# Additive masks with 64 contraction rows, first loads in four groups, and reordered stage transitions in a two-layer decoder with experts

## The chip, the cores and the metric

The kernel runs on one core of a Trainium2 chip. The metric is the device time of one execution in microseconds (us), as the median over several runs. The core has a matrix engine (TensorE, in the profile PE for products and PEld for weight loads), a vector engine (DVE), a scalar engine (ACT), GpSimd (POOL) and a queue that issues transfers (SyncE, SP). The matrix engine has two clock levels, 1.2 and 2.4 GHz, and the profile gives the granted one as a share of 2.4 GHz.

## What is computed

The input x has 8 items of 128 tokens with 256 features. Six sublayers follow each other, each of the form x = layernorm(x + f(x)); the kernel calls them A to F:

```python
x = _layernorm(x + _L0_attn_ref(x, ...))       # A: causal self-attention, 16 heads of 16
x = _layernorm(x + _L0_xattn_ref(x, ctx, ...)) # B: cross-attention on relu(linear) features
x = _layernorm(x + _L0_ffn_ref(x, ...))        # C: 64 experts of 96 units, top 8
x = _layernorm(x + _L1_attn_ref(x, ...))       # D: gated linear attention in chunks of 64
x = _layernorm(x + _L1_xattn_ref(x, ctx, ...)) # E: 32 query heads, 8 key heads, windows
x = _layernorm(x + _L1_ffn_ref(x, ...))        # F: 8 experts of 176, top 2, and a shared one of 704
```

Two of them mask their scores. A sets scores above the diagonal to minus infinity. E lets a query see two windows of keys, one of 64 tokens in one set of keys and one of 32 in the other, beside a linear bias:

```python
delta = -rel                                   # rel = key position - query position
ssm_mask = (delta >= 0) & (delta < W_SSM)      # 64
att_mask = (delta >= 0) & (delta < W_ATT)      # 32
scores = scores + bias[None]
scores = jnp.where(mask[None, None], scores, -jnp.inf)
wei = jax.nn.softmax(scores, axis=-1)
```

## The kernel before, in words

All activations stay on the chip. Each engine has its own program, written out by hand, and the engines meet on semaphores. A wait on an engine holds everything behind it on that engine. What is issued first is decided by the order of the calls in these programs.

**First loads.** The SP queue issues every transfer at L346, in lists called A, A2, B. A holds the whole transposed input (1 MB), a small head mask, all eight weights and biases of A, and two tensors of constants for `v` (a column of ones per head, 256 KB each); A2 holds the mask of A, two identities, the input by rows (1 MB). `loaded(engine, "A")` waits for the whole list: TensorE, ACT, DVE and POOL all begin with it.

**A and B** (`pe_self_cross`) are one software pipeline over 16 items: eight of A and then eight of B. Per step, TensorE projects keys, values and queries of one item, forms the scores of it (`scores`, L479 and L485), transposes the exponentials of another (L493), and multiplies with the values (L524). In A, `scores` first writes the mask into four PSUM banks: four products of the identity (128x128, bf16) with `causal` (512 columns), L479. The sixteen score products of 32 contraction rows at four tile positions (L485) accumulate onto it.

**C and F** (`pe_moe`) run over blocks of 128 hidden units: 48 in C and 17 in F. One block is `gate_up` (L995: for each half t of the tokens, a gate part s=0 and an up part s=1, six products of 512 columns each) and `down` (L1012: twelve products, six for each t). POOL splits each weight block into a high and a low part (L1977, L1979). Ahead of the loop the router decides the weights of the tokens: `pe_logits` (L960), a chain of small DVE instructions (`Router`), `pe_combine_T` (L970) for each half of the tokens, a copy by ACT into `cT`, and `pe_token_weights` (L981), which spreads them. As soon as both halves of `cT` are there, the SP queue writes them to DRAM, reads them back spread, issues the loads of all weights and constants of D and E (L320, in C only), and only then refills the four buffers of weight blocks (L284). Before its first `down`, TensorE clears the four output banks with products of the identity and a tile of zeros (L1030, four of 512 columns, bf16).

**D and E** (`pe_linear_cross`). D runs over eight items in 64x64 and 128x64 tiles. E then runs in iterations t of 12 steps k. In one iteration TensorE works for one item on `scores` (rows are queries, for the maxima that DVE takes) and for the item before it on `scores_T` (rows are keys, for the exponentials by ACT). Each call writes one PSUM bank of 512 columns: a mask product first (the identity with a mask, 128 contraction rows, bf16: L788 and L796 in `scores`, L829 and L836 in `scores_T`), and score products of 100 or 102 contraction rows on top. Every third step is a short one for the early queries: in `scores` four products of 128 columns (L792), in `scores_T` two of 256 (L832). The other eight steps have two products of 256 columns in each call (L799, L840). The order within a step is mask, scores, mask, transposed scores. Both calls run in seven of the nine iterations; the first has only `scores`, the last only `scores_T`.

## Time and profile before

| | |
|---|---|
| Median of 3 runs | 1089.61 us (1089.28 to 1089.79) |
| Profiled execution | 1087.74 us, of which the span from first to last instruction 1085.9 us |
| TensorE products | busy 993.8 us (92% of the span), 6139 instructions |
| TensorE weight loads | busy 785.1 us (72%), beside the products |
| DVE, ACT, POOL | busy 617.8, 430.2, 319.8 us |
| Mean granted clock of TensorE | 0.96 |
| Chain that ended last | TensorE 81%, transfers issued by SP 5%, DVE 5%, waiting for nothing visible 3% |

A product is shown with its contraction rows and output columns of the array (128\*128), its moving operand (128x512) and its type. Products are pipelined, and the profile models their ends; so two products are compared by their starts. A product of 512 columns of bf16 in a run of its own kind starts 0.216 us after the one before. Lines of code are lines of the kernel before.

### The profile page before, as it was taken

What the parts mean: (1) busy time and instruction counts of PE and PEld (TensorE: products, weight loads), DVE (VectorE), ACT (ScalarE), POOL (GpSimd) and SP (SyncE); (2) the same over time, 40 slices, a digit from 0 to 9 for tenths busy, and PEclk for the clock granted to TensorE, in tenths of its full rate; (3) what the DMA queues carried; (4) which work ended last, traced back from release to release, by engine and by line L of the source; (5) the groups of instructions that cost most, each with busy time, mean ns of one, the idle gap of its engine ahead of it and who ended that gap; (6) DMA issues with size and microseconds to landing.
All of it is one profiled execution on the core that took longest, in us unless ns stands there. A gap on an engine that the chain in (4) does not pass through costs nothing.

```text
span 1085.9 us, 18386 instructions
## 1 busy us (share of the span) xinstructions
PE 993.8 (92%) x6139; PEld 785.1 (72%) x6148; DVE 617.8 (57%) x1035; ACT 430.2 (40%) x839; POOL 319.8 (29%) x530
## 2 busy tenths in 40 slices
PE   4999997969999999999999689868999998999994
PEld 3778885658888888888888335557787776688883
DVE  2666777435555555555556457554555563455555
ACT  2777785413223223223222223224555554323221
POOL 0033124214443443443444301110000014234431
PEclk9999998989999999999999789978999999899998
DMA  8000000464333333333330000011111101264511
GB/s 298 2 2 2 2 2 2 94 177 140 129 115 117 110 111 119 107 110 120 109 106 15 9 1 1 17 27 27 25 25 31 32 11 59 59 183 106 120 31 39
DMA packets 36950, 75.74 MB, mean 70 GB/s; under 512 B 6844, under 2 KB 17960, under 8 KB 36498
## 3 DMA queue, kind: packets, MB, share of 16 engines
q1 hardware_dynamic: 36606, 74.77, 23.8%
q8 instruction: 34, 0.56, 0.2%
q0 software_dynamic: 288, 0.23, 0.2%
q14 instruction: 22, 0.18, 0.1%
HBM read 67.80 MB, written 2.40 MB: 65 GB/s over the span
## 4 chain that ended last, share of the span: by engine, by line
PE 81%; SPq 5%; DVE 5%; issue 3%; DMA 2%; ACT 2%; POOL 1%; DVEq 0%; POOLq 0%; ACTq 0%
PE ps L995 31%; PE ps L1012 15%; PE ps L411 4%; PE ps L628 3%; PE ps L418 3%; PE ps L493 3%; SPq L364 2%; SPq L320 2%; PE ps L861 2%; PE ps L485 2%; PE ps L524 2%; PE ps L745 1%; PE ps L836 1%; PE ps L840 1%; PE ps L796 1%
## 5 line engine op out<-in xcount | busy, mean ns | idle before, releaser
L995 PE MATMUL ps<-shared 128*128 128x512 f32 x1560 | 381.2, 394 | 9.5 <-POOL shared L1979 9.5
L995 PEld LDWEIGHTS ps<-shared 128*128 128x128 f32 x1560 | 296.9, 191 | 74.0 <-issue 11.7
L1397 ACT ACTIVATE shared<-pT 128x512 fp32r<-128x512 f32 x130 | 82.1, 632 | 287.4 <-DVE pT L1815 287.4
L1977 POOL CAST shared<-wraw 128x512 fp32r<-128x512 f32 (+1 forms) x130 | 92.0, 708 | 315.1 <-PE ps L1012 288.5
L1818 DVE TENSOR_TENSOR al<-pT,shared 128x512 fp32r<-128x512 f32 x130 | 117.1, 901 | 104.3 <-ACT shared L1397 104.3
L1012 PE MATMUL ps<-shared 128*128 128x512 f32 x520 | 162.4, 394 | 1.3 <-DVE al L1818 1.2
L1807 DVE TENSOR_TENSOR e<-e,ps 128x512 f32<-128x512 f32 x130 | 89.3, 687 | 128.4 <-PE ps L995 128.1
L1979 POOL TENSOR_TENSOR shared<-wraw,shared 128x512 fp32r<-128x512 f32 (+1 forms) x130 | 132.3, 1017 | 10.4
L1873 POOL TENSOR_SCALAR newton<-agg 128x1 f32<-128x1 f32 (+1 forms) x36 | 9.1, 254 | 384.1 <-DVE agg L1442 357.5
L1012 PEld LDWEIGHTS ps<-shared 128*128 128x128 f32 x520 | 98.4, 190 | 23.4 <-DVE al L1818 2.1
L1391 ACT ACTIVATE e<-ps 128x512 f32<-128x512 f32 x130 | 77.7, 597 | 84.3 <-PE ps L995 84.2
L1815 DVE TENSOR_TENSOR pT<-e,kbd 128x512 f32<-128x512 f32 x130 | 99.0, 761 | 10.0 <-DMA kbd<-combine_C 3.0
L1012 PE MATMUL ps<-al,shared 128*128 128x512 f32 x260 | 101.8, 392 | 0.0
L1012 PEld LDWEIGHTS ps<-al,shared 128*128 128x128 f32 x260 | 49.2, 189 | 10.3
L1458 DVE TENSOR_REDUCE mx<-ps 128x8 f32<-128x1024 f32 x32 | 39.0, 1220 | 22.2 <-PE ps L485 22.2
L1653 DVE TENSOR_REDUCE mcol<-ps 128x2 f32<-128x512 f32 x64 | 43.2, 677 | 6.0 <-PE ps L799 5.7
L411 PE MATMUL ps<-c_x_t,arena 128*128 128x128 f32 x192 | 28.2, 291 | 14.4 <-DMA v<-in_A_ones_v 12.4
L1137 ACT ACTIVATE pT<-ps 128x512 f32<-128x512 f32 x64 | 36.4, 598 | 8.0 <-PE ps L493 7.9
L799 PE MATMUL ps<-kT,shared 100*128 100x256 f32 x128 | 39.4, 391 | 0.0
L1466 DVE TENSOR_TENSOR e<-ps,mx 128x1024 f32<-128x1024 f32 x32 | 39.0, 1220 | 0.6
L411 PEld LDWEIGHTS ps<-c_x_t,arena 128*128 128x128 f32 x192 | 24.5, 197 | 20.3 <-DMA v<-in_A_ones_v 12.4
L1289 ACT ACTIVATE e<-ps 128x512 f32<-128x512 f32 x48 | 28.4, 595 | 26.6 <-PE ps L832 14.9
(225 smaller groups left out, 1447.5 us busy)
## 6 DMA issues: line engine op xcount, KB each, us to landing
kbd<-combine_C SPq DMA_DIRECT2D x46, 512.0 KB
wraw<-in_C_w SPq DMA_DIRECT2D x48, 384.0 KB, 8.1
kbd<-combine_F SPq DMA_DIRECT2D x15, 512.0 KB
wraw<-in_F_w SPq DMA_DIRECT2D x17, 384.0 KB, 7.1
kbd<-kbd SPq DMA_DIRECT2D x96, 32.0 KB, 1.9
kT<-kbd SPq DMA_DIRECT2D x48, 32.0 KB, 1.8
c_x_t<-in_x_t SPq DMA_DIRECT2D x1, 1024.0 KB, 4.9
c_x_rows<-in_x_rows SPq DMA_DIRECT2D x1, 1024.0 KB, 7.0
```

What stands on the lines that cost most here:

```text
L411: mm = pe.matmul(dst[:, c * P:(c + 1) * P], w[:, k, c * P:(c + 1) * P], src[:, k, :], start=(k == 0), stop=(k == C - 1))
L799: mm = pe.matmul(bank[:, o * D:(o + 1) * D], q_[0:KR, g, 1, o * P:(o + 1) * P], k_[t][0:KR], start=False, stop=True, skip_group_check=True)
L995: mm = pe.matmul(GU[t][s], w[u][:, (c * 2 + s) * P:(c * 2 + s + 1) * P], xx[:, c, t * HALF:(t + 1) * HALF], start=(i == 0), stop=(i == 5))
L1012: mm = pe.matmul(Y[:, 2 * m + t, :], w[u][:, (4 + m) * P:(5 + m) * P], x_[t][:, :], start=False, stop=False, skip_group_check=True)
L1391: act.activation(sgt[t], GU[t][0], ACT.Silu).then_inc(S("silu"), 1)
L1397: act.activation(ah[t][:, :], a2[t], ACT.Copy).then_inc(S("ah"), 1)
L1653: dve.reduce_max(m4[:, g0 + k % 3 - 1, 1, :], SRING[n % 2].rearrange("p (o k) -> p o k", o=2), AX.X)\
L1807: dve.tensor_tensor(a1[t], sgt[t], GU[t][1], ALU.mult).then_inc(S("m_a1"), 1)
L1815: dve.tensor_tensor(a2[t], a1[t], wbc[k][:, t * HALF:(t + 1) * HALF], ALU.mult)\
L1818: dve.tensor_tensor(al[t][:, :], a2[t], ah[t][:, :].bitcast(F32), ALU.subtract)\
L1977: pool.tensor_copy(wh[u][:, lo:hi], wraw[k][:, lo:hi]).then_inc(S("m_wh"), 1)
L1979: pool.tensor_tensor(wl[u][:, lo:hi], wraw[k][:, lo:hi], wh[u][:, lo:hi].bitcast(F32), ALU.subtract).then_inc(S("m_wl"), 1)
```

## The change

1. **Masks of E.** A mask product now contracts over 64 rows. Its stationary operand is 64x128 from a new constant `windows`, its moving operand 64 rows. The masks of `scores` lie on partitions 0 to 63 (tile position (0, 0)), those of `scores_T` on 64 to 127 (tile position (64, 0)). `scores` and `scores_T` are cut in halves h of 256 columns in the eight long steps. The order within a half is: mask of scores, mask of scores_T, score product, transposed score product. Per long step there are two pairs of masks of 256 columns, per short step one pair of 512.
2. **Masks of A.** Four products of 128 rows become eight of 64 rows and 64 output columns, at tile positions (0,0), (64,64), (0,64), (64,0).
3. **First loads** in groups A0 (input of two items, head mask, keys' weight and bias), A1 (values, queries), A2 (masks, identities, input rows of two items, output weight), A3 (the rest of the input). TensorE, ACT and DVE begin on A0, and wait for the later groups where they use them. The constants of `v` are no longer loaded; POOL writes them with four memsets. The biases of B are formed at step 6, not 2.
4. **Transitions.** Into C, the gate part of block 0 is issued a step earlier; the rest of `gate_up` of block 0 is spread around `pe_combine_T(1)`, which comes after 12 products and not after 24 (in F after 6, not 24). The clearing products of L1030 go: the first product into each bank starts it. The first `down` waits for two copies of token weights, not four. ACT is reordered to match.
5. Four mask tensors of E become one, so the SP queue issues three loads fewer at L320.

The diff, cut to its core:

```diff
-        XT = const("A", "x_t")
-        hmask = const("A", "head_mask")
-        causal = const("A2", "causal_bf16", BF16)
+        XT = sb("c_x_t", [P, C, T])
+        loads["A0"] = [(XT[:, :, 0:2 * P], a["x_t"][:, :, 0:2 * P])]
+        hmask = const("A0", "head_mask")
+        causal = [const("A2", f"causal{h}_bf16", BF16) for h in range(2)]
...
-        X = const("A2", "x_rows")
+        X = sb("c_x_rows", [P, B, D])
+        loads["A2"].append((X[:, 0:2, :], a["x_rows"][:, 0:2, :]))
+        loads["A3"] = [(XT[:, :, 2 * P:], a["x_t"][:, :, 2 * P:]), (X[:, 2:, :], a["x_rows"][:, 2:, :])]
...
-        for layer, names in (("A", "wq wk wv bq bk bv wo bo"),
-                             ("B", "wfc bfc wq wk wv bq bk bv wr"),
+        for group, names in (("A0", "wk bk"), ("A1", "wv bv wq bq"), ("A2", "bo wo")):
+            for n in names.split():
+                weight("A", n, group)
...
-        smask = [const("E", f"smask{h}_bf16", BF16) for h in range(2)]
-        tmask = [const("E", f"tmask{h}_bf16", BF16) for h in range(2)]
+        windows = const("E", "windows_bf16", BF16)
...
                     for r in range(4):
-                        pe.matmul(ps[:, r, :], ident16[:, :], causal[:, :], start=True, stop=False, skip_group_check=True)
+                        for n in range(2):
+                            rows, out = bass.ds(64 * n, 64), 64 * (n ^ r % 2)
+                            pe.matmul(ps[out:out + 64, r, :], ident16[rows, rows], bc(causal[r % 2][rows, :], 1, 4),
+                                      start=True, stop=False, tile_position=(64 * n, out), skip_group_check=True)
...
+                if t == 2 * B + 3:
+                    pe.wait_ge(S("pc"), 8 * B)
+                    pe_gate_up(pe, "C", 0, 0, 0, (0,))
...
-                    pe.wait_ge(S("pc"), 8 * B)
-                    pe_gate_up(pe, "C", 0, 0, 0)
...
+            def scores_mask(b, k, h):
...
+                if k % 3 == 0:
+                    pe.matmul(SRING[n % 2], windows[0:64, 0:P], bc(windows[0:64, P:2 * P], 1, 4),
+                              start=True, stop=False, tile_position=(0, 0), skip_group_check=True)
+                else:
+                    pe.matmul(SRING[n % 2][:, h * D:(h + 1) * D], windows[0:64, 0:P], windows[0:64, 2 * P:4 * P],
+                              start=True, stop=False, tile_position=(0, 0), skip_group_check=True)
...
+                lo, n_q, at_ = (0, 8, 0) if k % 3 == 0 else (P + h * P, 4, h * D)
+                pe.matmul(TRING[n % 3][:, at_:at_ + n_q * 64], windows[64:128, lo:lo + P],
+                          bc(ident16[64:128, 64:128], 1, n_q), start=True, stop=False, tile_position=(64, 0),
+                          skip_group_check=True)
...
-                    if es is not None:
-                        scores(es, k)
-                    if ev is not None:
-                        scores_T(ev, k)
+                    for h in range(1 if k % 3 == 0 else 2):
+                        if es is not None:
+                            scores_mask(es, k, h)
+                        if ev is not None:
+                            scores_T_mask(ev, k, h)
+                        if es is not None:
+                            scores(es, k, h)
+                        if ev is not None:
+                            scores_T(ev, k, h)
...
-            gate_up(0, 0, 1)
-            gate_up(1, 1, 0)
+            if L == "C":
+                pe_gate_up(pe, L, 0, 0, 0, (1,))
+            pe_gate_up(pe, L, 0, 0, 1, (0,))
             pe_combine_T(pe, BEFORE[L], 1)
+            pe_gate_up(pe, L, 0, 0, 1, (1,))
             pe_token_weights(pe, L, 0, 1)
             pe_token_weights(pe, L, 1, 1)
-            before_done(pe, L)
-            pe.wait_ge(S("zero16"), 1)
-            pe.wait_ge(S("m_spread"), 4 * (L == "F") + 4)
-            for m in range(4):
-                pe.matmul(Y[:, m, :], ident16[:, :], zero16[:, :], start=True, stop=False, skip_group_check=True)
+            gate_up(1, 1, 0)
+            pe.wait_ge(S("m_spread"), 4 * (L == "F") + 2)
             down(0, 0, 0)
             gate_up(1, 1, 1)
+            before_done(pe, L)
+            pe.wait_ge(S("m_spread"), 4 * (L == "F") + 4)
             down(0, 0, 1)
...
-            loaded(pool, "A")
+            for u in range(2):
+                pool.memset(v[u][:, :], 0.0).then_inc(S("v_one"), 1)
```

## Rows read from the trace of the kernel before

**Rows 1.** The page: its first line.
```profile
span 1085.9 us, 18386 instructions
```
**Rows 2.** Stages: length, busy (count) of PE, PEld, DVE, ACT, POOL; clock, DMA, GB/s.
```profile
811.00:834.00 23.00, 21.63 (x196) 17.93 (x195) 13.33 (x27) 12.38 (x25) 2.61 (x6) 1.00 0.13 29
...
907.00:945.00 38.00, 31.39 (x142) 21.71 (x143) 18.16 (x70) 13.15 (x30) 14.66 (x29) 0.87 0.16 30
```
**Rows 3.** Timeline of PE in E: start, length, line, tiles, shape, count [idle before].
```profile
801.89 0.38 PE L788 MATMUL ps<-c_smask_bf,c_ident_bf 128*128 128x512 bf16 x1
...
802.98 0.39 PE L796 MATMUL ps<-c_smask_bf,c_ident_bf 128*128 128x512 bf16 x1
...
803.91 0.39 PE L796 MATMUL ps<-c_smask_bf,c_ident_bf 128*128 128x512 bf16 x1
...
804.38 0.39 PE L836 MATMUL ps<-c_tmask_bf,c_ident_bf 128*128 128x512 bf16 x1
```
**Rows 4.** The same view in A, from masks to score products.
```profile
64.08 0.81 PE L479 MATMUL ps<-c_causal_bf,c_ident_bf 128*128 128x512 bf16 x3
64.82 0.71 PE L485 MATMUL ps<-kbd,qT 32*128 32x256 f32 x8
```
**Rows 5.** The same view in D, around a product of 33 contraction rows.
```profile
656.42 0.44 PE L671 MATMUL ps<-c_ident,an 128*128 128x128 f32 x2
656.79 0.50 PE L626 MATMUL ps<-shared 33*128 33x512 f32 x1
657.22 1.13 PE L628 MATMUL ps<-arena,c_x_t 128*128 128x512 f32 x2
```
**Rows 6.** A mask after a wait in E: its weight load, and its product.
```profile
757.61 0.10 PEld L788 LDWEIGHTS ps<-c_smask_bf,c_ident_bf 128*128 128x128 bf16 x1 [0.58 <-issue]
...
757.64 0.38 PE L788 MATMUL ps<-c_smask_bf,c_ident_bf 128*128 128x512 bf16 x1 [0.37 <-DMA kT<-kbd]
```
**Rows 7.** Waits in 811 to 834 us: total, times, longest.
```profile
PE ps L788 <- DVE shared L1637: 1.4, 1, 1.4
```
**Rows 8.** The chain that ended last: start, length, what.
```profile
6.31 6.07 DMA v<-in_A_ones_v
12.42 2.09 PE ps L411 x8
...
200.69 0.45 PE ps L970 x4
...
229.92 5.92 DMA wraw<-in_C_w
...
272.73 2.72 PE ps L995 x12
```
**Rows 9.** Transfers issued: source, queue, count, KB, us from issue to landing.
```profile
c_x_t<-in_x_t SPq DMA_DIRECT2D x1, 1024.0 KB, 4.9
```
**Rows 10.** Timeline of PE, DVE and SP into C.
```profile
184.94 0.69 PE L567 MATMUL ps<-c_ident,c_x_rows 128*128 128x128 f32 x2 [2.11 <-DVE c_x_rows L1518]
...
186.13 4.97 PE L995 MATMUL ps<-shared 128*128 128x512 f32 x12
...
196.51 0.42 DVE L1798 TENSOR_TENSOR oT<-oT,einv 128x256 f32<-128x256 f32 x1
...
227.44 0.90 SPq L320 DMA_DIRECT2D c_smask_bf<-in_smask_bf  x2
...
228.38 1.08 SPq L320 DMA_DIRECT2D c_tmask_bf<-in_tmask_bf  x2
...
238.26 4.55 PE L995 MATMUL ps<-shared 128*128 128x512 f32 x12 [9.49 <-POOL shared L1979]
```
**Rows 11.** Timeline of PE into F.
```profile
924.17 7.36 PE L995 MATMUL ps<-shared 128*128 128x512 f32 x24
...
935.80 1.49 PE L1030 MATMUL ps<-zero,c_ident_bf 128*128 128x512 bf16 x3 [1.16 <-ACT kbd L1381]
...
943.17 0.62 PE L1012 MATMUL ps<-shared 128*128 128x512 f32 x2
```

More of the change, by code:

```diff
@@ L65, in build, with weight @@
         filled = {"AB": 0, "DE": 0}
-        def weight(layer, name):
+        def weight(layer, name, group=None):
             src = a[f"{layer}_{name}"]
@@ L126, in build @@
         mx = [sb(f"mx{u}", [P, 8]) for u in range(2)]
-        for u in range(2):
-            loads["A"].append((v[u], a["A_ones_v"]))
         v3 = [x[:, :].rearrange("p (h w) -> p h w", w=VW)[:, :, 0:DH0] for x in v]
@@ L346, in load_weights @@
                     sp.dma_start(t[tuple(slice(None) for _ in t.shape)], src).then_inc(S(f"{L}_loaded"), 16)
-            load_weights("A")
-            load_weights("A2")
+            for group in ("A0", "A1", "A2", "A3"):
+                load_weights(group)
             load_weights("B")
@@ L794, in scores @@
                 else:
[L795 to L801 removed]
+                    mm = pe.matmul(bank[:, h * D:(h + 1) * D], q_[0:KR, g0 + k % 3 - 1, 1, h * P:(h + 1) * P],
+                                   k_[t][0:KR], start=False, stop=True, skip_group_check=True)
+                if k % 3 == 0 or h == 1:
+                    mm.then_inc(S("E_sps"), 1)
             def maxima_T(b, r):
@@ L834, in scores_T @@
                 else:
[L835 to L842 removed]
+                    mm = pe.matmul(bank[:, h * D:(h + 1) * D], k_[t][0:KM, (1 - h) * P:(2 - h) * P],
+                                   q_[0:KM, g0 + k % 3 - 1, 1], start=False, stop=True, skip_group_check=True)
+                if k % 3 == 0 or h == 1:
+                    mm.then_inc(S("E_sts"), 1)
             def values(b, r):
@@ L990, in pe_gate_up @@
                 pe.wait_ge(S("m_a1"), nm(L, 2, x * 2 + t - 1))
-            for s in range(2):
+            for s in parts:
                 i = 0
@@ L1010, in down @@
                 for m in range(C):
-                    for w, x_ in ((wh, ah), (wl, ah), (wh, al)):
+                    for i, (w, x_) in enumerate(((wh, ah), (wl, ah), (wh, al))):
                         mm = pe.matmul(Y[:, 2 * m + t, :], w[u][:, (4 + m) * P:(5 + m) * P],
-                                       x_[t][:, :], start=False, stop=False, skip_group_check=True)
+                                       x_[t][:, :], start=(first(x) and i == 0), stop=False, skip_group_check=True)
                 mm.then_inc(S("m_down"), 1)
@@ L1891, in residual @@
                     loaded(pool, "A2")
+                if L == "A" and b == 2:
+                    loaded(pool, "A3")
                 if L == "B" and b == 0:
@@ L1900, in residual @@
                     .then_inc(S("xb"), 1)
-            loaded(pool, "A")
+            for u in range(2):
+                pool.memset(v[u][:, :], 0.0).then_inc(S("v_one"), 1)
+            pool.wait_ge(S("v_one"), 2)
+            for u in range(2):
+                pool.memset(v[u][:, :].rearrange("p (h w) -> p h w", w=VW)[:, :, DH0:DH0 + 1], 1.0).then_inc(S("v_one"), 1)
             residual(0)
@@ L2022, in constants @@
     c["head_mask"] = (np.arange(P)[:, None] % 32 // DH0 == np.arange(2)[None, :]).astype(np.float32)
-    c["causal_bf16"] = bf16(np.tile(np.where(k > q, big, np.float32(0)), (1, 4)))
+    causal = np.where(k > q, big, np.float32(0))
+    c["causal0_bf16"], c["causal1_bf16"] = bf16(causal), bf16(np.roll(causal, 64, 0))
     def window(q, tokens, width):
```

116 lines of the change are left out of this document (52 added, 64 removed).

## The prediction, made before the change was run

> **What bounds the kernel now.** I read the table of stages first, then the chain that ended last, then the waits in E, then the timeline of TensorE where the change touches it. TensorE is the bound nearly everywhere: 81% of the chain is on it, and in an iteration of E (23 us) it is busy 21.6 us [rows 2]; the only wait of a product there that counts is 1.4 us, at the first short step [rows 7]. So an edit of TensorE's stream in A or E is worth what it does to that stream. There are three exceptions. The kernel begins with 12.4 us in which TensorE waits for list A of the loads; the last of its transfers was issued at 6.31 us and took 6.07 us [rows 8]. In C, TensorE stands still for 9.49 us until POOL has split a refilled weight block, and what POOL waits for hangs on the SP queue, which began its work when both halves of `cT` were there [rows 8, 10]. Into F there are small waits and a low clock: 0.87 over 38 us [rows 2, 11]. The span is 1085.9 us [rows 1], the profiled execution 1087.7 us, the median 1.9 us above that; the sum is made on the span, and the same difference is added to 1089.6.
>
> **Masks of E, the large term.** Before, a call's half of a step (one mask, 512 columns, and two score products of 256) takes 0.47 us (803.91 to 804.38) [rows 3]. Score products run at 0.227 us for 512 columns [rows 8], so the two take 0.24 and the mask 0.23. A long step with both calls takes 0.94 us. If a pair of masks in opposite halves of the rows runs at once, as four products at other tile positions do (L485, eight of them inside 0.71 us) [rows 4], a step saves one mask, 0.23 us.
>
> Against this stands the switch between tiles. The last causal mask starts at 64.08 + 2 x 0.216 = 64.51 and streams until 64.73; the first product of 32 rows, and its weight load with it, begin only at 64.82: 0.09 us in which nothing flows, though no wait is shown [rows 4]. The same holds where only the rows differ: L626, with 33 contraction rows, starts at 656.79 and L628, with 128, at 657.22: 0.43 us for a product that takes 0.227 in a run of its kind, so 0.20 for the switch [rows 5]. The way into L626 costs 0.09 too: the second product of L671 starts about 0.17 after the first and streams 0.11, to 656.69 [rows 5]. The 0.20 splits into 0.09 of standing still and 0.11 of a weight load that is otherwise hidden. A bf16 mask's weights come quicker: product 0.03 after its load [rows 6]. So the way into a mask costs 0.12, the way out 0.20. Score products have 100 and 102 rows and so use the whole array; before, mask and scores were of one kind and none of this was paid.
>
> The Trainium skill says the same in "TensorEngine Tiling (Array Packing)", section Tiling Modes: changing the mode, not just the tile, drains the engine. The trace agrees, with 0.09 us each time [rows 4, 5]. The same page's Overview gives up to 2 times for a contraction of at most 64; by that alone the masks would halve, which is the first rival below.
>
> Long step, per half h, after: 0.12 into the masks, 0.11 for the pair of 256 columns, 0.20 out of them, 2 x 0.117 for a score product of each call: 0.665 us; two halves 1.33, so 0.39 more than 0.94. Short step: before 1.09 (801.89 to 802.98) [rows 3]; after 0.12 + 0.22 + 0.20 + 4 x 0.11 + 0.235 = 1.21, so 0.12 more. An iteration with both calls: 8 x 0.39 + 4 x 0.12 = 3.6 us. Off this go 0.3, because in three places the stream changes tiles next to a mask already (values twice, keys and values once), and 0.4, because the 1.4 us of waiting [rows 7] hangs on a DVE chain that starts with the short step k=9 and has longer to run: 2.9 us each, 7 x 2.9 = 20.3. The last iteration has only one mask per pair, so nothing is saved: a long step of `scores_T` goes from 0.47 to 2 x (0.12 + 0.107 + 0.20 + 0.117) = 1.09, a short one gains 0.30: 8 x 0.61 + 4 x 0.30 = 6.1, less 0.7 of switches and waits that are there already: 5.4. In the first iteration TensorE waits for DVE and for transfers of the next keys anyway; only what is ahead of these keys counts: 2.0. Sum for E: **+27.7 us**. Bounds: a mask's weight load with 64 rows is not in the trace; between 0.03 and the 0.11 of the other kind this adds up to 0.08 for each of 160 groups of masks, 12 us. Downward, DVE and ACT have slack and could hide nothing more of a TensorE stream than the waits already in it; I allow 8 us for these. E lies between +19 and +41. New waits are added too: the transposed mask's wait for ACT stands ahead of the score product that DVE needs. Banks come round two and three steps later, so I cost it at nothing; what hides it is ACT's 12.4 busy of 23 us [rows 2], and a price would be at most some 0.3 us a step.
>
> **Masks of A.** Before 4 x 0.216 = 0.86 us per item [rows 4]. After, if all four tile positions run at once, 0.09 + 0.06 + 2 x 0.213 = 0.58; the way on to L485 costs what it did. 8 x 0.27 = **-2.1 us**. Here two tiles of different rows write one bank, which no row shows: with one after the other it is 8 x 0.213 + 0.1 = 1.8, so +7.6 us at the other end. I take the first, as L485 shows tiles together [rows 4].
>
> **First loads.** A0 is 0.5 MB in four transfers, issued by 2.7 us. The 1 MB of x_t was there 4.9 us after its issue at 0.9 us [rows 9], so half of it is there at about 5 us, and TensorE starts at 5.0 instead of 12.4: **-7.4 us**. A1 is needed 1.9 us after the start, but queries wait for ACT anyway. A2 (fifteen transfers in, some 2 MB) lands near 10.5, needed near 11. A3 has 7 us to spare. If A1 or A2 is late, up to 3 us are given back. POOL's four memsets lie in the time of loading. Moving the biases of B takes away a DVE wait that would otherwise have appeared; nothing gained.
>
> **Into C.** The end is set by the SP queue, so what counts is when the second half of `cT` is written. Before, `pe_combine_T(1)` ran at 200.69 [rows 8], though its DVE input was ready at 196.93 [rows 10]. After, 12 products fewer stand ahead (2.7), and six were moved into the 2.11 us hole before 184.94, out of the group that ran at the low clock (4.97 for twelve) [rows 10]; that brings the router's DVE chain forward by some 1.5 us, so the input is ready near 195.4 and the transposes run at about 196: 4.6 us sooner. Behind it the four mask loads took 2.0 us to issue [rows 10]; one is left: 1.4. The refill at 229.92 [rows 8] and the product at 238.26 [rows 10] move by **-6.0 us**. The clearing products of C cost nothing already: the wait of 9.49 behind them grows by what they free. Bounds -3 and -7.
>
> **Into F.** Here TensorE sets the pace. Before, from 924.17 to 943.17, it did 24 + 6 + 12 products of 512 columns in 19.0 us, with the clearing, a wait of 1.16 [rows 11] and one of 0.7 for `cT`, half of it at the low clock. The 24 took 7.2 us up to the next group where 24 x 0.227 is 5.4, so some 8 went at half speed, 3.4 us. After, the waits are covered by products: the same 3.4 us for the first 8, then 34 x 0.227 = 7.7, and 2.8 for transposes and token weights (0.6, and four long products at 0.43 with their switches): 13.9: **-5.1 us**. If the clock drops as before, 2 less. Bounds -2 and -6.
>
> **Sum.** -7.4 - 2.1 - 6.0 - 5.1 + 27.7 = +7.1. Span 1093.0, median 1089.6 + 7.1 = 1096.7 us.
>
> **Rivals.**
> 1. *The switch is not paid around masks of 64 rows.* Then E saves 0.23 for each of 84 pairs of masks, -19.3, and the total is -40: 1050 us. For it: nothing in the rows. Against it: 0.09 at every change of rows or columns [rows 4, 5]. It decides at the first pair: half a step would take 0.36, not 0.67.
> 2. *E loses less and the rest gains all it can* (not slower): each iteration pays 1.9 instead of 2.9 because the waits of 1.4 us [rows 7] vanish wholly, and C and F give 7 and 6: +19 - 22.5 = -3.5 to -6: 1085 us. It turns where E costs less than 20.6 us.
> 3. *Masks' weight loads take 0.11, or the masks of A go one by one*: +7 to +12 more: 1106.
> 4. *Less flows per microsecond in E and the clock falls.* A tenth of the 200 us of E at the low clock would add most of 20 us: 1115. Against it: it was 1.00 in 811 to 834 [rows 2].
>
> **How the numbers follow.** Forecast 0.61, own range 1087 to 1105. Rival 1: 0.14. Rival 2: 0.12. Rival 3: 0.10. Rival 4: 0.03. The range 1079 to 1111 takes in rival 3 and most of rival 2, and leaves out rival 1 and the far end of 4. A measurement can tell 0.2% or 2.2 us, so faster is below 1087.4 and slower above 1091.8. Faster: rival 1 and 0.11 of rival 2, 0.25; same: 0.01 of rival 2 and 0.11 of the forecast, 0.12; slower: the rest of the forecast 0.50, rivals 3 and 4 0.13, together 0.63.
>
> **What would show it.** In the changed profile: a long step of E with both calls near 1.33 us from pair to pair, with 0.09 us of nothing before the masks' and the scores' weight loads; iterations of 26 us and not 23; TensorE's first product near 5 us; the product after the refill wait near 222.8 (7.4 + 2.1 + 6.0 before 238.26); one stretch of low clock into F where there were two. The prediction is wrong if a pair costs under 0.4 us with both ways, if the start is later than 8 us, or if the refill wait in C grows by what was gained ahead of it.

## The result and the profile after

The changed kernel takes 1117.07 us (median, 1111.67 to 1119.68), the kernel before 1089.44 beside it: a ratio of 1.0257 with a 95% interval of 1.021 to 1.0303. That is 27.6 us slower, where the forecast was 7.1 slower and the range ended at 1111. A second comparison gave 1.0264 (1.0235 to 1.0293). So the direction was right and the size was not.

The page of the changed kernel, its first lines (columns as in [rows 1, 2]; the last line is TensorE's granted clock in 40 slices):

```profile
span 1115.8 us, 18701 instructions
...
PE 1049.1 (94%) x6300; PEld 788.7 (71%) x6300; DVE 621.5 (56%) x1034; ACT 432.6 (39%) x839; POOL 319.9 (29%) x534
...
PEclk9999996989999999999998699779889998899998
```

The span by stage shows where the time went. Each line is one stretch: its length, then busy time and count for PE, PEld, DVE, ACT and POOL, then the clock, the share of DMA, GB/s. The five stretches are: first product to the first token weights (A and B); from there to D's first numerators (C); to the products of keys and values in E's first iteration with scores, some 8 us behind its first mask (D); to the first token weights of F (E); and to the last products (F). The kernel before:

```profile
12.40:192.80 180.40, 170.21 (x1705) 138.25 (x1712) 121.31 (x208) 127.78 (x275) 47.03 (x128) 0.98 0.08 28
192.80:639.40 446.60, 422.51 (x1802) 337.15 (x1803) 244.32 (x346) 131.18 (x217) 174.16 (x214) 0.96 0.34 103
639.40:717.00 77.60, 67.83 (x447) 40.23 (x448) 52.69 (x95) 22.42 (x56) 10.42 (x36) 0.93 0.04 9
717.00:922.30 205.30, 185.14 (x1558) 150.41 (x1556) 109.25 (x236) 100.91 (x211) 29.25 (x72) 0.97 0.12 30
922.30:1073.30 151.00, 147.74 (x630) 118.97 (x632) 82.56 (x126) 47.95 (x80) 54.45 (x65) 0.97 0.38 90
```

The changed kernel:

```profile
5.58:186.40 180.82, 171.70 (x1739) 138.66 (x1739) 121.48 (x207) 127.86 (x275) 47.22 (x128) 0.97 0.11 39
186.40:634.40 448.00, 428.01 (x1805) 340.35 (x1804) 244.37 (x346) 131.43 (x217) 173.02 (x213) 0.95 0.35 102
634.40:712.70 78.30, 69.53 (x448) 40.36 (x449) 52.73 (x95) 22.42 (x56) 10.43 (x36) 0.92 0.03 9
712.70:955.70 243.00, 233.44 (x1684) 151.92 (x1682) 112.86 (x235) 103.08 (x211) 29.23 (x72) 0.89 0.09 26
955.70:1103.20 147.50, 146.08 (x627) 117.34 (x628) 82.71 (x126) 47.85 (x80) 54.38 (x65) 0.98 0.38 92
```

The first product comes 6.8 us sooner (12.4 to 5.58). E takes 37.7 us more, at a clock of 0.89 where it was 0.97. F takes 3.5 less. C, which was to gain 6, gains nothing (446.6 and 448.0). A second profiled execution of the changed kernel showed 0.89 in E too.

Three of E's iterations, as windows (columns as before); [rows 2] has 23.00 us at a clock of 1.00 for the same work:

```profile
793.39:821.97 28.58, 27.75 (x213) 18.32 (x212) 13.85 (x27) 12.60 (x26) 2.61 (x6) 0.88 0.09 23
821.97:849.20 27.23, 26.40 (x212) 17.49 (x212) 13.84 (x27) 12.61 (x26) 2.61 (x6) 0.94 0.10 24
849.20:876.47 27.27, 26.44 (x212) 17.50 (x212) 13.83 (x27) 12.60 (x26) 2.61 (x6) 0.94 0.10 24
```

The timeline of PE (TensorE's products) within E, halves of a long step (start, length, line, tiles, shape). L798 and L842 are the two masks, L812 and L856 the score products of the two calls:

```profile
786.41 0.39 PE L798 MATMUL ps<-c_windows_bf 64*128 64x256 bf16 x1
...
787.47 0.39 PE L798 MATMUL ps<-c_windows_bf 64*128 64x256 bf16 x1
...
806.51 0.28 PE L798 MATMUL ps<-c_windows_bf 64*128 64x256 bf16 x1
806.52 0.28 PE L842 MATMUL ps<-c_ident_bf,c_windows_bf 64*128 64x256 bf16 x1
806.73 0.39 PE L812 MATMUL ps<-kT,shared 100*128 100x256 f32 x1
806.95 0.28 PE L856 MATMUL ps<-shared,kT 102*128 102x256 f32 x1
807.16 0.28 PE L798 MATMUL ps<-c_windows_bf 64*128 64x256 bf16 x1
```

The two masks of a pair start 0.01 us apart, so they do run at once. From pair to pair it is 0.65 us (806.51 to 807.16), where the prediction had 0.665 and the kernel before 0.47 [rows 3]. The first two lines are the same half step inside a stretch of low clock: 786.41 to 787.47, 1.06 us. By the windows above, each of these iterations now has such a stretch, of 6.8 us at first and of 3 to 4 in the later ones; before, the clock was 1.00 there.

### The profile page after: what moved, and what is told of

Same layout as the page of the kernel before. It is cut to its first block, busy times and chain, and to the rows that moved or that the text cites. A ratio compares the mean times of both kernels' runs of the same rounds, so it can differ in the third digit from the quotient of the medians.

```text
span 1115.8 us, 18701 instructions
## 1 busy us (share of the span) xinstructions
PE 1049.1 (94%) x6300; PEld 788.7 (71%) x6300; DVE 621.5 (56%) x1034; ACT 432.6 (39%) x839; POOL 319.9 (29%) x534
## 4 chain that ended last, share of the span: by engine, by line
PE 85%; DVE 5%; SPq 4%; issue 2%; DMA 2%; ACT 1%; POOL 1%; DVEq 0%; POOLq 0%; ACTq 0%
PE ps L1017 30%; PE ps L1034 15%; PE ps L411 4%; PE ps L636 3%; PE ps L812 3%; PE ps L878 3%; PE ps L500 3%; PE ps L418 2%; PE ps L798 2%; PE ps L492 2%; SPq L320 2%; PE ps L809 2%; PE ps L531 2%; PE ps L856 2%; SPq L364 1%
## 5 line engine op out<-in xcount | busy, mean ns | idle before, releaser
L812 PE MATMUL ps<-kT,shared 100*128 100x256 f32 x128 | 53.3, 416 | 0.0
L842 PE MATMUL ps<-c_ident_bf,c_windows_bf 64*128 64x256 bf16 (+1 forms) x160 | 49.9, 312 | 1.4 <-DMA shared<-mlo 1.4
L1313 ACT ACTIVATE e<-ps 128x512 f32<-128x512 f32 x48 | 28.7, 598 | 40.5 <-PE ps L856 23.4
L1313 ACT ACTIVATE pT<-ps 128x512 f32<-128x512 f32 x48 | 28.7, 597 | 35.1 <-PE ps L856 21.2
L856 PE MATMUL ps<-shared,kT 102*128 102x256 f32 x128 | 39.5, 308 | 0.0
L500 PE MATMUL ps<-c_ident,e 128*128 128x128 f32 x256 | 38.3, 285 | 1.2 <-ACT pT L1161 0.8
```

Source lines behind the costliest of these rows:

```text
L500: mm = pe.transpose(PT[h][:, q * P:(q + 1) * P], e[u][:, at_:at_ + P], ident[:, :])
L812: mm = pe.matmul(bank[:, h * D:(h + 1) * D], q_[0:KR, g0 + k % 3 - 1, 1, h * P:(h + 1) * P], k_[t][0:KR], start=False, stop=True, skip_gro ...
L856: mm = pe.matmul(bank[:, h * D:(h + 1) * D], k_[t][0:KM, (1 - h) * P:(2 - h) * P], q_[0:KM, g0 + k % 3 - 1, 1], start=False, stop=True, sk ...
```

## Experiments

Every version stands beside the kernel before on the same chip. The first four were on a chip where the kernel before took 1087.60 us, the next four (the parts alone and the first of the versions with one change of tiles per long step) on one where it took 1087.18, the other four on one where it took 1085.13. Ratios are to these, with 95% intervals.

### Without E's masks

```diff
-    windows = const("E", "windows_bf16", BF16)
+    smask = [const("E", f"smask{h}_bf16", BF16) for h in range(2)]
+    tmask = [const("E", f"tmask{h}_bf16", BF16) for h in range(2)]
...
-    for h in range(1 if k % 3 == 0 else 2):
-        ... scores_mask, scores_T_mask, scores, scores_T
+    if es is not None: scores(es, k)
+    if ev is not None: scores_T(ev, k)
```

> The changed kernel with the masks of stage E, and the order of their products, as they were before the change; the loads in groups, the transitions and the masks of stage A as changed. Theory: all of the loss is in E, where the trace of the changed kernel shows +38.4 us between the start of E's loop and F; without it 1117.07 - 38.4 = 1078.7 us, 10.7 below before, and the middle iterations of E take 23.0 us again. Rival 1, the rest gains the whole of what the prediction summed (20.6 us) and E's masks interact with it: 1069 us. Rival 2, part of the loss belongs to the new transitions (a shifted phase of the clock into E): 1085 us or more, with E's iterations above 23.5 us.

Measured: 1070.26 us, ratio 0.9826 (0.9796 to 0.9857). E is back at its old length, so the loss sits in E's masks and the order of their products:

```profile
709.80:915.20 205.40, 185.23 (x1558) 150.49 (x1556) 109.23 (x235) 100.94 (x211) 29.25 (x72) 0.97 0.12 30
```

The rest gains 18.9 us by the ratio, which lies at rival 1's value (20.6) more than at the theory's 10.7. The profiled execution, 1075.5 us, was the slowest of its five, and by its stages it gains 12.2.

### E's masks alone

The reverse: the kernel before with the changed code of `windows`, `scores_mask`, `scores`, `scores_T_mask`, `scores_T` and the loop over halves.

> The kernel before with the new masks of stage E and the new order of their products alone. Theory (price of the switch between kinds of tiles, and the lower granted clock that follows in E): +38 us, 1127 us, middle iterations of E at 27 to 29 us, of which some 2 to 3 us of difference come with each stretch of low clock. Rival, the switch's price alone, as the prediction had it: +27.7, 1117 us, middle iterations near 26 us.

Measured: 1126.19 us, ratio 1.0333 (1.0297 to 1.037), 36.2 us slower. E by stages:

```profile
725.70:969.50 243.80, 236.37 (x1683) 154.67 (x1681) 112.11 (x235) 103.05 (x211) 29.29 (x72) 0.88 0.10 26
```

243.8 us, as in the changed kernel (243.0). From the first mask of one iteration to that of the next it is 30.3, 27.2, 27.2 and 27.3 us, 28.0 in the mean; in the changed kernel the same four take 28.6, 28.6, 27.2 and 27.3, 27.9 in the mean. (The profiled execution, 1135.6 us, was the slowest of six, 9 us above the median. Its A and B took 185.9 us where they had taken 180.4; its E agrees with the changed kernel's.) The rest of the change has no part in E's loss. The theory's 38 holds, the prediction's 27.7 does not.

### The new order and halves with masks of 128 rows

```diff
-    pe.matmul(SRING[n % 2][:, h * D:(h + 1) * D], windows[0:64, 0:P], windows[0:64, 2 * P:4 * P],
-              ..., tile_position=(0, 0), ...)
+    pe.matmul(SRING[n % 2][:, h * D:(h + 1) * D], ident16[:, :], smask[1][:, :], ...)
```

and so for the transposed masks.

> The changed kernel with its order and its halves, but the masks of E as products of 128 rows from the whole array (same count of instructions, same columns, the old tensors). Theory, the price lies in the switch between products of 64 rows and of more: no stop of 0.09 us before a weight load, half a long step 0.45 to 0.47 us, iterations 23 to 23.4 us, 1078 to 1081 us in all. Rival, the price lies in the order (a mask and its product apart, four weight loads in place of pairs): half a long step stays at 0.65 us, iterations at 27 us, 1115 us.

Measured: 1081.91 us, ratio 0.9933 (0.9904 to 0.9963). E and one half step (the same four products as above; mask to mask 816.38 to 816.85):

```profile
708.70:924.10 215.40, 194.76 (x1683) 155.53 (x1681) 110.41 (x235) 100.90 (x211) 29.37 (x72) 0.93 0.12 29
```

```profile
816.38 0.28 PE L799 MATMUL ps<-c_smask_bf,c_ident_bf 128*128 128x256 bf16 x1
816.50 0.27 PE L843 MATMUL ps<-c_tmask_bf,c_ident_bf 128*128 128x256 bf16 x1
816.53 0.36 PE L813 MATMUL ps<-kT,shared 100*128 100x256 f32 x1
816.73 0.28 PE L856 MATMUL ps<-shared,kT 102*128 102x256 f32 x1
816.85 0.28 PE L799 MATMUL ps<-c_smask_bf,c_ident_bf 128*128 128x256 bf16 x1
```

With as many products in the same order, half a step takes 0.47 us again: here the masks follow one another, and still it is 0.18 quicker than with the two at once. So the price lies in going from masks of 64 rows to products of 100 or more and back. (The two versions also differ in the masks' tile position and tensors. The doubled pairs of the next run, where further masks of 64 rows cost about their columns, speak against a price of the masks by themselves.) The order is not wholly free, though: E is 10.0 us longer than without E's masks, at a clock of 0.93 and not 0.97, where two middle iterations held the full clock and took 23.4 us (0.4 more). What in the order lowers the clock elsewhere, the halves or the transposed mask's wait that now stands ahead of the scores, was not tried apart. Here too the low stretches in the middle of E, 781 to 784 and 853 to 856 us, stand right behind the wait at the head of an iteration (1.5 us), but behind three other such waits there is none.

### Each pair of masks twice

```diff
     scores_mask(es, k, h)
     scores_T_mask(ev, k, h)
+    if es is not None and ev is not None:
+        scores_mask(es, k, h)
+        scores_T_mask(ev, k, h)
```

> The changed kernel with each pair of E's mask products issued twice in a row, where scores and transposed scores both run (the second pair writes the same values again; no further switch of tiles, 0.107 us more of columns per half of a long step, 0.21 per short step, 1.9 us per iteration at full clock, 7 iterations). Theory, the low clock in E comes with the share of time in which TensorE stands between the tiles: more columns per switch hold the clock up, iterations near 27.2 us all, +1 to +6 us on the changed kernel: 1118 to 1123 us. Rival, the low clock comes from the one long wait at the start of each iteration alone: it stays as it is and the columns come on top, +14 us or more at the mixed clock: 1131 to 1134 us.

Measured: 1121.02 us, ratio 1.0303 (1.027 to 1.0336), and one of E's iterations:

```profile
815.60:843.50 27.90, 27.51 (x252) 17.46 (x251) 13.79 (x27) 12.59 (x25) 2.61 (x6) 1.00 0.09 24
```

The expectation miscounted the columns added: an iteration has eight long steps and four short ones, so it is 8 x 2 x 0.107 + 4 x 0.213 = 2.6 us and not 1.9. Seven iterations would then cost 18 us; by the two ratios they cost 4 (1.0303 against 1.0264). The clock is why: it stands at 1.00 in every iteration from the third on, where the changed kernel had 0.88 to 0.94. An iteration here is 28.0 us, of which TensorE waits 0.4. So 27.6 less 2.6, and the 0.8 that it waits in the changed kernel, make some 25.8 us for an iteration of the changed kernel at full clock; it took 27.2 to 28.6. This run changes two things at once: it adds columns, and as these give VectorE more time, it also halves the wait at the head of the iteration (0.83 to 0.39 us). Which of the two holds the clock it can't say; the rival, that the clock stays low and the columns come on top, fell.

### The parts alone

The kernel before with the loads in groups alone, with the two transitions alone, and with A's masks alone.

> The kernel before with its first loads in four groups (and the ones in v written by POOL) alone. Theory: TensorE starts 6.4 to 6.8 us sooner and keeps it, as no later wait takes it up: -6.5 us against the kernel before. Rival, the gain is taken back by the wait for the second group and for the masks' load within the first items: -3 us or less.

Measured: 1079.43 us, ratio 0.9929 (0.9903 to 0.9955): -7.7 us. The first product is at 6.25 us, 6.2 sooner than before; the interval, -10.5 to -4.9, is too wide to tell 7.7 from that.

> The kernel before with the reordered transitions into C and F alone. The prediction had -6.0 (into C) and -5.1 (into F), -11.1 us. Theory, from the trace of the changed kernel, where stage C's steady loop began no more sooner than the first loads and the masks of A account for, and F came out 3.5 us shorter: -5 us, all of it in F, because into C the freed time is spent at low clock and on the weights' transfer. Rival, the prediction's terms were right and the change in E's masks hid them: -11 us, with both stages shorter by 5 to 6 us.

Measured: 1083.25 us, ratio 0.998 (0.995 to 1.001): -2.2 us, between -5.4 and +1.1. Its stretches of A with B, of C, and of F:

```profile
12.10:198.20 186.10, 175.86 (x1706) 142.22 (x1706) 121.50 (x207) 127.78 (x275) 46.97 (x128) 0.94 0.07 27
198.20:639.90 441.70, 422.09 (x1805) 338.16 (x1804) 244.72 (x346) 131.49 (x218) 173.41 (x213) 0.97 0.35 104
...
921.40:1069.00 147.60, 146.06 (x626) 117.03 (x627) 82.93 (x128) 47.93 (x81) 54.44 (x65) 0.98 0.39 92
```

F is 3.4 us shorter. A to C together take 627.8 us, before 627.0: nothing was gained into C. The end of B ran at a lower clock here, 0.65 over 170 to 195 us; in the kernel before it was 0.86. A mean as low is no mark of the new order: with E's masks alone, whose instructions in B are those of before, it was 0.55 (in the slowest of its six executions). The time from the first product to the first write of `cT` to DRAM was 189.4, 189.7, 195.0 and 189.0 us in the four profiled kernels with the old transition. In the ten profiled executions with the new one it lay between 186.5 and 195.3, with a median of 188.7; nine of these have A's new masks too, worth some 2, and their median is 187.7. So this stretch differs by several us from one execution to the next, and the reordering gives next to nothing, not the 4.6 of the prediction.

> The kernel before with the new masks of stage A alone. The prediction had -2.1 us (8 items, 0.28 us each). Theory, from the trace of the changed kernel (0.63 us for the eight products in place of 0.86): -1 to -2 us. Rival, the other end of the prediction's bounds, where the products of 64 rows do not run beside each other or the clock falls: +5 us.

Measured: 1085.47 us, ratio 0.9984 (0.9963 to 1.0005): -1.7 us, which is the prediction's -2.1 within what can be told, but by the interval (-4.0 to +0.5) no gain at all is possible too; the timeline, shown further down, decides.

### One change of tiles per long step

```diff
-    for h in range(1 if k % 3 == 0 else 2):
-        if es is not None: scores_mask(es, k, h)
-        if ev is not None: scores_T_mask(ev, k, h)
+    if es is not None: scores_mask(es, k, 0)      # 512 columns
+    if ev is not None: scores_T_mask(ev, k, 0)    # two products of 256
+    for h in range(1 if k % 3 == 0 else 2):
         if es is not None: scores(es, k, h)
         if ev is not None: scores_T(ev, k, h)
```

> The changed kernel with the masks of a whole long step (512 columns of each) ahead of its products, one change of tile kinds per step where there were two. Theory, the loss in E goes with the number of changes between kinds: per both-iteration 6 x (0.97 - 0.94) + 3 x 0.12 = +0.5 us at full clock, +3 us in the last iteration, +1 in the first, and 0 to 10 us of low clock as in the version with 128 rows: 1078 to 1090 us, middle iterations near 23.6 us. Rival, the loss comes from products of 64 rows as such (their own duration or their weight loads), not from the changes: as much as in the changed kernel, 1113 us or more, middle iterations at 27 us.

Measured: 1106.94 us, ratio 1.0186 (1.0156 to 1.0216). In this version the mask of one half of the transposed scores is lost. So it was run once more with the second transposed mask product as `start=(at_ == 0)`, which keeps it.

> As whole_steps, one change of tile kinds per long step, but the second of the two products that write a transposed mask doesn't begin its bank anew. Theory: a product that begins anew lets the products after it write over what the same bank's other half held, so in whole_steps one mask was lost, with no effect on time; here it is kept, and the time is the same: 1105 to 1109 us, E's iterations 23.6 us plus half of the low clock's 6.8 us. Rival: the lost mask was a sign of products that ran into each other, and the time changes with it by 5 us or more.

Measured: 1103.77 us, ratio 1.0167 (1.0137 to 1.0196), and an iteration of E:

```profile
815.50:842.40 26.90, 25.48 (x203) 17.18 (x203) 13.64 (x27) 12.29 (x26) 2.61 (x6) 0.87 0.10 25
```

So a product that starts its bank anew decides how later products treat what stands elsewhere in that bank, and the time hardly changes (3 us by the medians, on two chips, intervals that overlap). The Trainium skill, "PSUM — Partial Sum Buffer", section The four PSUM rules, states it so: the region that a starting product resets is the whole 2 KB bank, whichever part it writes; the two versions here agree with it. Neither theory of the first expectation holds whole: 1078 to 1090 us was expected if the loss went with the number of changes, 1113 or more if it did not. The loss falls by 8 to 11 us (1.0264 to 1.0186 and 1.0167) with half of the long steps' changes of tiles gone. At full clock the iteration would be 26.9 less half of the 6.8 us of low clock that it holds, 23.5, as expected (8 x 0.03 + 4 x 0.12 more than 23.0 is 23.7). But the clock is 0.87, no better than with twice as many changes: TensorE stands at the head of the iteration for 1.42 us (26.90 less 25.48), where it is 0.83 in the changed kernel. That the longer wait, together with the changes of tiles that remain, is what keeps the clock down is argued from this, and not tried in this version.

### The wait at the head of an iteration, filled

The waits of PE in the changed kernel, 780 to 900 us (line, releaser: total in us, times, longest):

```profile
PE ps L795 <- DVE shared L1664: 4.2, 5, 0.8
```

Each iteration begins with one wait of 0.8 us for VectorE's masked queries ([rows 7] had 1.4), and the low clock begins at it or up to some 2 us behind it, in all five iterations. The timeline and the window that follow show the first of the five:

```profile
784.80 0.37 PE L795 MATMUL ps<-c_windows_bf 64*128 64x512 bf16 x1 [0.83 <-DVE shared L1664]
```

```profile
785.90:792.70 6.80, 6.80 (x42) 3.10 (x41) 3.04 (x5) 1.94 (x4) 0.19 (x1) 0.50 0.02 5
```

The experiment puts four products of 512 columns ahead of that wait; their output is written over by the mask.

```diff
     if k == 0:
+        for _ in range(4):
+            pe.matmul(SRING[n % 2], ident16[:, :], bc(ident16[:, :], 1, 4), start=True, stop=False, ...)
         pe.wait_ge(S("E_k0st"), b * 48 + 48)
         pe.wait_ge(S("E_qm"), b * 2 + 1)
```

> The changed kernel itself, beside the next three on one chip. Theory (the parts add up: -18.9 us without E's masks, +36.2 for E's masks alone): ratio 1.016 to 1.02. Rival (the parts make each other worse by a further 10 us, as 1117.07 against 1070.26 us has it): ratio 1.025 or more.

Measured: 1112.64 us, ratio 1.0264 (1.0235 to 1.0293), which is +25.5 to +31.8 us. The theory's 1.016 to 1.02 fell; the number is the rival's, but not for its reason, since the four parts alone add up to -7.7 - 2.2 - 1.7 + 36.2 = +24.6, just below this interval and each with an interval of its own (2 to 4 us to either side). It is the version without E's masks that stands out by 7 us against the sum of its own three parts (-18.9 against -11.6, with intervals that just meet); nothing in its trace names a cause.

> The changed kernel with four products of 512 columns (0.85 us, written over afterwards) issued ahead of the wait with which each iteration of E begins (0.5 to 0.9 us, for VectorE's masked queries). Theory: the lower clock in E comes with the share of time that TensorE stands, and this wait is where that share is largest; filled, the clock holds as in the version with doubled pairs, the iterations take 25.5 us, and 7 x 1.7 = 12 us are gained less up to 3 for products that outlast the wait: 1104 to 1110 us where the changed kernel takes 1117. Rival: the stops at the changes of tiles alone are enough to lower the clock; iterations stay at 27 to 28.5 us, no gain or up to 3 us lost: 1115 to 1120.

Measured: 1100.09 us, ratio 1.0133 (1.0107 to 1.016), 12.5 us less than the changed kernel beside it, with 32 products more. One iteration (the next took 25.70 us too), and the whole of E with the fill and, from the execution of the changed kernel beside it, without:

```profile
785.40:811.10 25.70, 25.70 (x216) 17.26 (x215) 13.82 (x27) 12.59 (x25) 2.61 (x6) 1.00 0.10 26
...
711.80:939.10 227.30, 223.50 (x1711) 147.07 (x1709) 112.61 (x235) 102.84 (x211) 29.21 (x72) 0.97 0.10 28
```

```profile
707.60:950.00 242.40, 233.73 (x1684) 153.15 (x1682) 112.25 (x236) 103.06 (x211) 29.49 (x72) 0.89 0.10 26
```

The clock is 0.97 over E, as it was before the change, and E is 15.1 us shorter. This separates the two parts of E's loss: 22.0 us (227.3 - 205.3) for the switches, and 15.1 for the clock. Both are differences between single profiled executions, good to a few us. Not tried was the same filling elsewhere in the iteration; so that the wait is covered, and not only that more columns flow, rests on the wait's place right ahead of each low stretch.

### The refill ahead of the loads of D and E

The version without E's masks, in which SP issues C's first four refills of weights before the loads of D and E and not after them:

```diff
-    for M in ("D", "E"): ...            # loads of D and E, 21 transfers
+    for k in range(NW):
+        refill(1, k)
+    for M in ("D", "E"): ...
-    with sp.Fori(1, BLOCKS[L] // NW) as j:
+    with sp.Fori(1 + (L == "C"), BLOCKS[L] // NW) as j:
```

> The version without E's masks (no_e_masks) in which SP issues stage C's first four refills of weights ahead of the loads of D and E, instead of behind them. Theory: what the reordered transition into C could gain is taken by TensorE's wait of 9.2 us for the refill, which stands behind 22 to 25 us of those loads' issues on SP's queue; with the refill ahead the wait goes, and so 5 to 9 us: 1061 to 1065 us where no_e_masks takes 1070. Rival: the refill waits for VectorE, ScalarE or POOL to free the buffer, or for the transfer itself, and the order on SP changes nothing: 1070 us; or D's weights now come late, 1072 us or more.

Measured: 1062.33 us, ratio 0.9789 (0.9749 to 0.9828). The SP queue into C in the version without E's masks, from D's first load to the refill, and the product that waits for its data:

```profile
198.44 0.34 SPq L321 DMA_DIRECT2D arena<-in_D_wqk  x1
...
221.23 0.35 SPq L285 DMA_DIRECT2D wraw<-in_C_w  x1
...
229.26 5.44 PE L1004 MATMUL ps<-shared 128*128 128x512 f32 x12 [9.17 <-POOL shared L1998]
```

and with the refill ahead, with C's stretch:

```profile
201.41 0.35 SPq L285 DMA_DIRECT2D wraw<-in_C_w  x1
...
223.82 2.39 SPq L333 DMA_DIRECT2D arena<-in_D_wqk  x1
```

```profile
185.20:621.70 436.50, 421.25 (x1806) 338.02 (x1805) 244.94 (x345) 131.31 (x218) 173.82 (x213) 0.97 0.34 105
```

The refill goes out 19.8 us sooner, the wait of 9.17 is gone (one of 2.73 for a later block of weights takes its place), and C takes 436.5 us in place of 449.0. It is the quickest version of this study: 22.8 us less than the kernel before. Against the version without E's masks, run on another chip, the medians differ by 8 us while the intervals of the ratios overlap, so the step between the two rests on the traces.

## Why the prediction was wrong, point by point

**Switch between tiles (the kernel of the E term): right.** Half a long step was predicted at 0.665 us and took 0.65. With the wait filled, an iteration of 25.7 us holds 0.85 of filling; its work without that grew to 24.85 from the 21.63 of [rows 2], by 3.2, where the prediction had 3.3. Rivals 1 (no switch price) and 2 (E loses less) fell at the first pair, and rival 3 did too: mask weights cost no more than assumed, and A's masks run at once. (The 0.227 us that the prediction gives for score products is read from products of C [rows 8]; nothing in the sum turned on it.) For A, the timeline shows it, from the transposes ahead of the masks; before, with the score products at 64.82 [rows 4], and changed:

```profile
62.93 1.10 PE L493 MATMUL ps<-c_ident,e 128*128 128x128 f32 x8
```

```profile
65.57 1.10 PE L500 MATMUL ps<-c_ident,e 128*128 128x128 f32 x8
66.60 0.63 PE L485 MATMUL ps<-c_causal_bf,c_ident_bf 64*64 64x512 bf16 x8
67.15 1.15 PE L492 MATMUL ps<-kbd,qT 32*128 32x256 f32 x16
```

From the start of the transposes to the first score product it was 1.89 us and is 1.58: 0.31 less per item where 0.27 was forecast. Eight products of 512 columns pass in the 0.55 us from the first mask to the first score product.

**The sum over iterations in E: somewhat high.** 27.7 was predicted at full clock, and 22.0 remain with the wait filled. By the starts of the first mask of each iteration, the first one (scores only) takes 26.7 us with the fill and took 24.7 before, 2.0 more as forecast. The last, transposed scores only, was forecast at +5.4 and took 4.9 more (15.1 to 20.0 us from the last score product to the last transposed one). The seven with both calls take 15.2 more together where 20.3 was forecast. The miss is in the first two of them, 24.8 and 25.4 us with the fill, 23.8 and 25.7 before: there the kernel before waits for transfers and runs some 7 and 3 us at the low clock, and the filled one hardly does either. The prediction granted such waits to the first iteration only.

**The clock in E: the step that failed.** The prediction read 1.00 in [rows 2] and took the clock as given, with 0.03 for rival 4, "less flows per microsecond in E and the clock falls". That is what happened: +15.1 us. The rival's mechanism and its price (most of 20 us) were right, its chance was not. The change takes columns out (one mask of two) and puts stops in; both are in the prediction's own sum, and the kernel before already had 1.4 us of waiting in each iteration [rows 7]. The sum counted the stops as time and not as idle TensorE. Doubled masks, with half of the wait, and a filled wait each brought the clock in E's middle back to 1.00 without taking one change of tiles away. The wait alone did not lower the clock in the kernel before, where it was longer (1.4 us). With masks of 128 rows in the new order, so without a stop at the tiles, it did (1.5 us) in some iterations. So the low clock follows the wait, and the changed stream around it makes it fall there; how much of that the stops at the tiles do is not shown.

**First loads, -7.4: right within what can be told.** -7.7 alone; the first product came at 5.58 us in the changed kernel and 6.25 with the loads alone, where 5.0 was forecast.

**Masks of A, -2.1: right.** -1.7 alone, and 8 x 0.31 = 2.5 us by the timeline above.

**Into C, -6.0: wrong, about 0.** Both terms of it failed. The first is "12 products fewer stand ahead (2.7)" of the last transposes of `cT`, with what follows from it, "4.6 us sooner". It took products at full clock that in the new order run at the low one. The chain that ended last, before and changed (start, length, what; the transposes stand next):

```profile
192.83 1.98 PE ps L981 x4
194.81 5.88 PE ps L995 x24
```

```profile
186.46 3.71 PE ps L1003 x4
190.16 5.40 PE ps L1017 x12
```

The four products of the token weights take nearly twice as long, and twelve products of 512 columns almost as long as 24 did. It is so in all ten profiled executions with the new order: 3.7 us for the four and 4.1 to 5.3 for the twelve, by their starts. In the four with the old order it is 1.9 for the four and 5.8 for the 24. The transposes were to run 0.6 us after their input was ready; they ran 3.6 us after it in each execution of the old order and 3.2 to 4.3 in those of the new. What makes the low clock stay on there was not tried.

The second term is the 1.4 us for three mask loads less. They do shorten the queue: from the write of `cT` to the issue of the refill it is 27.2 us in the mean of the six profiled executions that load four masks and 25.6 in the seven that load one. But the refill then takes 5.4 us to land in the former and 7.1 in the latter, so that it is there 32.7 us after the write in both.

The product behind the refill wait, forecast at 222.8 us, stands at 231.29, 7.0 us sooner than before, of which the earlier start is 6.8 (the changed kernel):

```profile
231.29 5.36 PE L1017 MATMUL ps<-shared 128*128 128x512 f32 x12 [7.28 <-POOL shared L2011]
```

The other half of the reading was right: the SP queue sets C's start, as the refill put ahead showed. What the prediction wrote as its own test, that it is wrong "if the refill wait in C grows by what was gained ahead of it", did not come true either: the wait went from 9.49 to 7.28 us, and nothing was gained ahead of it.

**Into F, -5.1: near.** 3.4 alone, 3.5 in the changed kernel, 5.1 without E's masks. The clock over the first 19.3 us of F was 0.82 in the changed kernel:

```profile
955.70:975.00 19.30, 19.30 (x63) 12.80 (x64) 10.79 (x33) 8.44 (x16) 5.26 (x8) 0.82 0.30 56
```

The waits are covered (PE is busy throughout) and there is one stretch of low clock where there were two, as forecast; but 0.82 over 19.3 us means some 7 us at half speed where the forecast had 3.4. That is the case which the prediction priced at 2 less, and it came out at 1.7 less.

**The sum.** By terms, predicted and measured: E +27.7 and +37 (22 of switches, 15 of clock); loads -7.4 and -7.7; A's masks -2.1 and -1.7; C -6.0 and about 0; F -5.1 and -3.5. The measured terms give +24, the comparison 27.6. The switches came out 5.7 us cheaper than forecast, which hid a part of the clock's 15.1; without that luck the miss would be larger still. The two large misses are one kind of mistake: both took the clock that the kernel before shows at a place as a constant of that place, while the change itself moved it.

## What to carry to other kernels

Count what a change does to TensorE's idle share, not only to its time: fewer columns together with more stops lowered the granted clock here, and then products that were not touched are slower too. Two masks at once in opposite row halves gain 0.11 us per pair of 256 columns here, and the way into the tile kind and out of it costs 0.3 together. So it pays only where many such products follow each other, or where tiles change at that place anyway, as in A, whose masks always stood beside products of 32 rows. Ahead of a steady loop, look at what stands in front of its first refill on the issuing queue before reordering the engine that waits for it.

## What the runs showed of the hardware

- Idle TensorE cost more than its time. Four superfluous products per iteration (0.85 us) in a wait of 0.8 us made the iteration 1.5 to 2.9 us shorter (27.2 to 28.6, then 25.7), with the granted clock at 1.00 in place of 0.88 to 0.94.
- Two products of 64 contraction rows in opposite halves, with all 128 columns each and different banks, start within 0.01 us of each other; eight of 64x64 tiles, of which two with different rows write into the same bank (into different halves of its partitions), take 0.55 us for 8 x 512 columns.
- A pair of masks of 64 rows between products of 100 and 102 rows (all with 128 columns of the array) makes half a step longer by 0.18 us (0.65 against 0.47) than masks of 128 rows one after the other, although it streams 256 columns less.
- The end of B, with the same instructions, ran at a mean clock of 0.86 in one execution and 0.55 in another (25 us each), and the write of `cT` came 5.6 us later after the first product (189.4 and 195.0 us).
- Three transfers fewer ahead of the refill on the SP queue let it go out 1.6 us sooner, and it landed no sooner: 32.7 us after the write of `cT` in both cases (means of six and seven profiled executions).
